# Node sweeps in chunks of four blocks instead of eight, in a graph network kernel on one core

## The reference: what is computed

```python
def _L0_gnn_ref(...):
    for l in range(N_LAYERS):                      # 3 rounds
        m = concatenate([x[dst], x[src], edge_features])
        m = _ffn(m, msg_w1[l], msg_b1[l]); m = _ffn(m, msg_w2[l], msg_b2[l])
        agg = segment_sum(m, dst, N_NODES)
        x = x + _ffn(concatenate([x, agg]), upd_w[l], upd_b[l])
def _ffn(x, w, b): return relu(_ln(x @ w + b))

h = maximum(_layernorm(x), 0.0)
x = x + _L0_gnn_ref(h, edge_attr_16, ...)
h = maximum(_layernorm(x), 0.0)
x = x + _L1_gnn_ref(h, edge_attr_32, ...)          # gates: z = [x_i, x_j, e] @ W_f, W_s
h = maximum(_layernorm(x), 0.0)
x = x + _L2_gnn_ref(h)                             # segment sum of h[src]
h = maximum(_layernorm(x), 0.0)
x = x + _L3_gnn_ref(h, edge_attr_32, ...)
```

## Time and profile before

| what | value |
|---|---|
| median of three runs | 10311.94 us |
| the profiled execution's own time | 10303.77 us |
| its span, first to last instruction | 10302.0 us |
| PE, DVE, ACT, POOL busy over the span | 75%, 65%, 60%, 68% |
| windows of the four sweeps | 54, 78, 78 and 124 us |

### The profile page before, as it was taken

How to read it: one execution, slowest core, us unless ns; L and a number is a source line. 1 busy time by engine, 2 the same in 40 slices (tenths; PEclk the granted TensorE clock), 3 DMA queues, 4 the chain that set the end, 5 groups by cost and what they waited for, 6 DMA issues and landing times. The chain is left out here.

```text
span 10302.0 us, 371177 instructions
## 1 busy us (share of the span) xinstructions
PE 7708.6 (75%) x123397; PEld 6597.2 (64%) x123398; DVE 6703.4 (65%) x15839; ACT 6194.6 (60%) x16024; POOL 7045.8 (68%) x9555
## 2 busy tenths in 40 slices
PE   7666666646578999889998899977777756455666
PEld 5444444434467888788887888866666646445666
DVE  7444444456635999737886378863499993664697
ACT  2555555546636999728996289962388852442343
POOL 2777777777746888657885478850188855774676
PEclk9999999985589999899998999989999989657887
DMA  6222222249999888597775977769988859667987
GB/s 250 67 67 68 70 66 66 67 150 327 326 274 312 273 278 274 171 363 253 240 239 143 372 245 239 239 109 384 369 264 257 255 158 360 208 206 237 317 288 218
DMA packets 1408418, 2335.54 MB, mean 227 GB/s; under 512 B 311979, under 2 KB 826300, under 8 KB 1381310
## 3 DMA queue, kind: packets, MB, share of 16 engines
q1 hardware_dynamic: 1078046, 1293.68, 40.3%
q0 software_dynamic: 217824, 515.78, 17.0%
q10 hardware_dynamic: 112320, 523.03, 12.7%
HBM read 1381.15 MB, written 905.59 MB: 222 GB/s over the span
## 5 line engine op out<-in xcount | busy, mean ns | idle before, releaser
L639 POOL DMA_INDIRECT by_src<-sort_rec,slots x1560 | 1543.9, 990 | 650.8 <-issue 650.8
L1328 POOL DMA_INDIRECT NEAR<-spread_f,gather_ids_l x1368 | 1375.9, 1006 | 252.2 <-issue 180.2
L1453 ACT ACTIVATE z_l<-z_l,sizes_l 128x64 f32<-128x64 f32 x5472 | 1376.9, 342 | 0.1
L773 PE MATMUL bank<-hots_t 104*128 104x512 bf16 (+3 forms) x1568 | 614.4, 467 | 720.4 <-ACT junk L598 720.2
L773 PEld LDWEIGHTS bank<-hots_t 104*128 104x128 bf16 x1568 | 218.3, 139 | 1020.0 <-ACT junk L598 832.5
L1536 PE MATMUL bank<-wm_diag,zr_t_l 128*128 128x128 f32 x5472 | 795.6, 288 | 2.6 <-issue 2.6
L1536 PEld LDWEIGHTS bank<-wm_diag,zr_t_l 128*128 128x128 f32 x5472 | 664.8, 192 | 158.7 <-issue 158.7
L1490 PE MATMUL bank<-m_l,hot_wide_l 128*128 128x64 f32 x5472 | 740.7, 278 | 0.0
L1183 POOL COPY unit_near_a<-NEARB 128x192 bf16 x1368 | 417.4, 349 | 424.9 <-PE bank_bf L1168 209.9
L1515 PE MATMUL bank<-NEARB,hot_t_l 128*128 x16416 | 644.5, 194 | 46.3 <-DMA hot_t_l<-dst_hots_t 15.6
L1490 PEld LDWEIGHTS bank<-m_l,hot_wide_l 128*128 128x128 f32 x5472 | 664.3, 192 | 0.0
(11 more groups left out here) (392 smaller groups left out, 27495.3 us busy)
## 6 DMA issues: line engine op xcount, KB each, us to landing
spread_f<-unit_rows_a ACTq DMA_DIRECT2D x342, 512.0 KB, 5.9
hot_t_l<-dst_hots_t SPq DMA_DIRECT2D x456, 256.0 KB
hot_wide_l<-dst_wide SPq DMA_DIRECT2D x456, 256.0 KB
unit_hot_a<-src_hots_t SPq DMA_DIRECT2D x342, 256.0 KB, 4.0
dst_hots<-NEAR SPq DMA_DIRECT2D x228, 256.0 KB
dst_hots_t<-hot_t_l SPq DMA_DIRECT2D x228, 256.0 KB
dst_wide<-hot_wide_l SPq DMA_DIRECT2D x228, 256.0 KB
NEAR<-dst_hots SPq DMA_DIRECT2D x456, 128.0 KB
```

What stands on the lines that cost most here:

```text
L639: pool.indirect_dma_start(out=by_src, out_offset=bass.IndirectOffsetOnAxis(ap=slots[h][:, j:j + 1], axis=0), in_=rec[h][:, j, :], in_offse ...
L773: pe.matmul(to, lhsT=cols[:, t * P:width], rhs=cols[:, 0:width], start=True, stop=False, skip_group_check=True)
L1328: pool.indirect_dma_start(out=far_in[h % WA][:, g * GT:(g + 1) * GT, :].rearrange("p j f -> p (j f)"), out_offset=None, in_=spread_f, in_o ...
L1453: last = act.activation(z[h % WA][:, t, :], z[h % WA][:, t, :], ACT.Relu, scale=sizes[h % WA][:, 2, 0, t:t + 1])
```

## The change

The sweeps use `QUADS`, chunks of four blocks: thirteen chunks (twelve of four, and a last one of one block). The lags, the order of parts in a tick, the number of slots and every wait stay. A sweep has 17, 19, 19 and 20 ticks. Every work buffer of the sweep is half as wide. The final stage of the kernel has its own loop over `CHUNKS` and keeps eight. After the change line numbers behind the two new lines are higher by two.

```diff
         WIN = 8
         CHUNKS = [(a, min(a + WIN, NW)) for a in range(0, NW, WIN)]
+        QUAD = 4
+        QUADS = [(a, min(a + QUAD, NW)) for a in range(0, NW, QUAD)]
...
                 if update:
-                    h_t, acc_t = tiles("h_t", [P, WIN // 2, P]), tiles("acc_t", [P, WIN // 2, P])
-                    t_pre, relu = tiles("t_pre", [P, WIN, D]), tiles("relu", [P, WIN, D])
-                square, centre = (x_[:].rearrange("p j f -> p (j f)")[:, 0:WIN * D].rearrange("p (w f) -> p w f", f=D)
+                    h_t, acc_t = tiles("h_t", [P, QUAD // 2, P]), tiles("acc_t", [P, QUAD // 2, P])
+                    t_pre, relu = tiles("t_pre", [P, QUAD, D]), tiles("relu", [P, QUAD, D])
+                square, centre = (x_[:].rearrange("p j f -> p (j f)")[:, 0:QUAD * D].rearrange("p (w f) -> p w f", f=D)
                                   for x_ in (stage, stage_t))
-                hn_t = tiles("hn_t", [P, WIN // 2, P])
-                near_sum, near_rest, far_rest = ([state[:, k * WIN * width:(k + 1) * WIN * width].rearrange(
+                hn_t = tiles("hn_t", [P, QUAD // 2, P])
+                near_sum, near_rest, far_rest = ([state[:, k * QUAD * width:(k + 1) * QUAD * width].rearrange(
...
                 def windows_of(i):
-                    a, b = CHUNKS[i]
+                    a, b = QUADS[i]
...
                 def ticks(tick):
-                    for t in range(len(CHUNKS) + last_lag):
-                        tick(lambda lag: t - lag if 0 <= t - lag < len(CHUNKS) else None)
+                    for t in range(len(QUADS) + last_lag):
+                        tick(lambda lag: t - lag if 0 <= t - lag < len(QUADS) else None)
...
                             if update:
-                                act.wait_ge(s["t_sum"], min(i + 2, len(CHUNKS)))
+                                act.wait_ge(s["t_sum"], min(i + 2, len(QUADS)))
```

## The result

The changed kernel takes 10290.56 us, the median of 21 runs, against 10310.07 us before beside it, the median of 21. The ratio is 0.9979, 95% interval 0.9972 to 0.9986. I had forecast 10356 us, in a range from 10326.

A forecast was written before the change was run, and what follows sets the result against it. Sweeps were taken as bound by waits between engines in a ring, with fixed costs paid per tick; losses of 8.4 + 17.6 + 18 = 44 us on 10303.77 gave 10348, and 8.2 to the median 10356 us, range 10326 to 10388.

The forecast's parts named there:

- Nothing outside the sweeps is changed: Whole kernel: with barriers before and after each sweep, whatever a sweep gains or loses goes into the time in full.
- all other stages as before: Profile after, outside the four sweeps: expected sign that no other stage's time moves.
- a stage behind a sweep changes: Stages after a sweep: listed as one sign that the prediction is wrong, with no size given.
- The sum of the sweeps: All four sweeps: losses of 8.4 + 17.6 + 18, together +44 us.
- Ticks: Sweeps' half-width ticks: 4.36 us for 6.72 in sweep 0, 5.83 for 9.73 in sweep 1, 9.3 for 14.83 in sweep 3.
- fill and drain: Sweeps' pipeline ends: same number of ticks but shorter, 39.2 to 25.5, 49.1 to 30 and 94.4 to 59 us.
- Sweep 3 was to lose 18: Sweep 3: from 122.6 to 141 us, with 0.9 us a full tick for POOL getting in DVE's way.
- Sweeps 1 and 2: Sweeps 1 and 2, same code: from 76.3 to 85 us, +8.8 us each.
- sweep 0 7.4 instead of 8.4: Sweep 0: from 52.6 to 61.0 us, +8.4 us.
- the 122.6 us of sweep 3: Sweep 3 before the change: length read from the timeline, 6838.98 to 6961.57.
- PE's clock: PE in the sweeps: stays mostly at its lower level, 1.2 GHz; the higher one throughout would give 33 us back.
- Pipelining: Rival for the sweeps: parts overlap so a tick of four costs half a tick of eight; 88 us less, 10224; 5%.
- The Trainium skill's rule that I weighed: Sweeps: breaking up instructions on an unsaturated engine that makes others wait would make them faster; the basis of the first rival.

The follow-up runs named there:

- after_dve_1: Changed kernel (quads everywhere) plus one idle semaphore raise on DVE behind sweep 3's last tick: 10307.97 us, ratio 0.9983.
- pad_pe_66: Unchanged kernel (eights) plus 66 idle semaphore raises on PE alone behind sweep 3's last tick: 10314.78 us, ratio 1.0000.
- after_pad_188: Changed kernel plus idle instructions behind sweep 3 bringing each engine's added count to whole multiples of 256 (188 more on DVE): 10381.19 us, ratio 1.0054.
- pad_dve_1: Unchanged kernel (eights) plus one idle semaphore raise on DVE behind sweep 3's last tick: 10257.04 us, ratio 0.9945.
- pad_256: Unchanged kernel (eights) plus 256 idle semaphore raises on each of DVE, ACT, POOL and PE behind sweep 3: 10354.32 us, ratio 1.0031.
- quads_012: Unchanged kernel with chunks of four in sweeps 0 to 2 only, sweep 3 in eights: 10279.64 us, ratio 0.9963.
- quads_3: Unchanged kernel with chunks of four in sweep 3 only: 10270.0 us, ratio 0.9956.
- pad_all: Unchanged kernel (eights) plus idle instructions behind sweep 3: 324 on DVE, 276 ACT, 120 POOL, 66 PE: 10289.58 us, ratio 0.9971.
- pad_mod: Unchanged kernel (eights) plus idle instructions behind sweep 3: 68 on DVE, 20 ACT, 120 POOL, 66 PE: ratio 0.9959, measured where sorting ran slower.
- pad_dve_68: Unchanged kernel (eights) plus 68 idle instructions on DVE alone behind sweep 3: ratio 0.9922, measured where sorting ran slower.

## Why the prediction was wrong

- **The step that failed: "Nothing outside the sweeps is changed", and with it "all other stages as before".** True of the work, not of the time. The change gave DVE 324 more instructions ahead of the gate pass; that moved its code by 68 beyond a multiple of 256, and the pass went from the slow pattern to the fast one, -59.4 us. The sweeps' 36.0 and the pass's -59.4 make -23.4, against -19.5 measured. With the place put back the loss is there: +58.7 with 23.0 of padding. The prediction had named "a stage behind a sweep changes" as a sign that it is wrong, but gave it no price and no chance.
- **The sum of the sweeps** was 44 and came out at 36.0, right in mechanism and 8 too large. Ticks: sweep 0 4.29 us (I had 4.36), sweep 1 5.80 and later 6.40 (5.83 and 6.4), sweep 3 9.2 and later 10.47 (9.3 and 10.8).
- **The mis-sized terms** lie in sweep 3 and in fill and drain. Sweep 3 was to lose 18 and lost 14.8: DVE's L1777, at 3.10 us once before, is 0.69 in most of its full ticks; what POOL's L1832 (1.36 us) costs there is a wait of 0.48 at L1793. Sweeps 1 and 2 lost 7.0 and 6.8 instead of 8.8, sweep 0 7.4 instead of 8.4. One reading was short: the 122.6 us of sweep 3 ends where its last instruction starts; with that one's 0.63 it is 123.2, and the loss 17.8.
- **PE's clock.** The forecast kept the lower level, and the granted clock fell further, from 0.57 to 0.52 in sweep 1. The reason given was wrong: PE's busy share did not fall but rose, from 49.09 of 78 us to 55.43 of 83.6, for the same 369 matmuls, which took longer each.
- **The rivals.** Pipelining does not win: no sweep got shorter. The Trainium skill's rule that I weighed ("Perfetto Trace Analysis", "Optimizing Scalar/DVE Operations", breaking up instructions where an engine isn't saturated) does not carry here: DVE is busy 33.97 of 83.6 us and the sweep is 7 us longer. Of my cases only this one, at 5%, was on the faster side, and for another cause; that the total came out faster at all was luck of place.
- **A sign that was there.** In the trace before, steps of the same code took 3.95 us for a stretch and 4.3 for most of it, and L2106 took 676 ns on average where 256 columns of such an operation cost 0.42. A pass with two speeds may change its speed with what stands ahead of it.

The message passes came out 12.5 us longer. Their code is the same in all these kernels, and yet the first pass ranges from 1080.9 to 1096.2 us where sorting ran at its usual speed; what sets that is open.

## What to carry to other kernels

A stage is not "as before" because its code is. Look for loops whose step has two lengths in one trace, name the instruction that differs, and put such a stage's whole spread into the range. And a change that wins a little should be run again with a few different counts of idle instructions ahead of the loops, before its gain is credited to what it does; a single one is not enough, as after_dve_1 shows.

## What the runs showed of the hardware that I had not expected

- **DVE stands still behind POOL when it reads two SBUF tiles.** L2106 beside a tensor instruction of POOL, or started 0.31 to 0.58 us behind the start of an indirect load, ends 0.27 to 0.29 us behind that instruction; in the first 0.3 us of the load it runs free (0.44 us at +0.02), and the additions, with one input in PSUM, run free beside the load (1.28 us for two). The Trainium skill, "SBUF — State Buffer", section "Who interferes with whom", says that a DVE instruction with two SBUF inputs contends with a GpSimd instruction that reads SBUF, and calls the port pair that they share an exclusive lock; the trace agrees, and adds that of an indirect load only a part does it.
- **The place of code counts, and moving it by 256 or 512 instructions changes nothing.** The page's part on queues has the fetches:

```profile
q8 instruction: 144, 2.36, 0.1%
q14 instruction: 84, 0.69, 0.0%
```

  That is 2.36 MB in 144 packets, 16.4 KB each, and 0.69 MB in 84, 8.2 KB each. The Trainium skill, "Runtime: NRT & Kernel Launch", section "Instruction fetch mechanics", gives 16 KiB blocks of 256 instructions and calls crossing one mostly hidden. The packets of q8 have that size, those of q14 half of it, and the runs fit 256 without singling it out. One wait goes with the place, and it is small: in before, DVE's first addition behind the turn of the loop starts 0.09 us later behind its L2106 than the others do, in 23 of 26 rounds of eight steps. The same wait is there in 23, 21 and 25 rounds of pad_pe_66, after_pad_188 and pad_dve_1, at 0.06 us in 22 rounds of pad_256, and in no round of the other seven kernels with the old order (the change, quads_012, quads_3, pad_all, pad_mod, pad_dve_68, after_dve_1).
- **A wait under half a microsecond is followed by the slow pattern.** In before, pad_pe_66, after_pad_188 and pad_256, and in no other of these, an addition in the step ahead of the turn is late as well, by 0.07 to 0.34 us, in some rounds whose steps take 3.95 us. Of their 16 slow stretches 15 begin one or two steps behind such an addition. The first in before (DVE and POOL rows):

```profile
7511.24 0.42 DVE L2106 TENSOR_TENSOR gate_piece<-gate_rest 128x256 bf16<-128x256 f32 x1
...
7511.91 1.29 DVE L2115 TENSOR_TENSOR gate_z<-bank,gate_far_in 128x512 f32<-128x512 f32 x2 [0.26 <-issue]
...
7515.52 0.97 POOL L2010 DMA_INDIRECT gate_far_in<-spread_g,gate_ids  x1 [0.16 <-issue]
...
7516.10 0.67 DVE L2106 TENSOR_TENSOR gate_piece<-gate_rest 128x256 bf16<-128x256 f32 x1
```

  and the same step in pad_dve_1, without the wait:

```profile
7512.81 0.42 DVE L2110 TENSOR_TENSOR gate_piece<-gate_rest 128x256 bf16<-128x256 f32 x1
...
7513.15 1.28 DVE L2119 TENSOR_TENSOR gate_z<-bank,gate_far_in 128x512 f32<-128x512 f32 x2
...
7517.09 0.97 POOL L2014 DMA_INDIRECT gate_far_in<-spread_g,gate_ids  x1 [0.16 <-issue]
...
7517.32 0.42 DVE L2110 TENSOR_TENSOR gate_piece<-gate_rest 128x256 bf16<-128x256 f32 x1
```

  Behind the wait L2106 starts 0.58 us behind the load and stands still; without it, 0.23 us behind, and it runs free. Shown is that the place decides, and that these waits come with the place. That they are late fetches of instructions is argued and not shown, and why pad_dve_1 has one slow stretch without the wait ahead of the turn is open.
